# Input rows of the last 27 expert tiles turned by a DMA instead of TensorE and VectorE

## What is computed

```python
def _L1_ffn_ref(x, Wr, Wg, Wu, Wd):
    logits = jnp.einsum('bsd,de->bse', x, Wr)
    topk_w, topk_idx = jax.lax.top_k(jax.nn.softmax(logits, axis=-1), 2)
    ...
    gate = jax.nn.silu(jnp.einsum('th,ehi->tei', xf, Wg))
    hidden = gate * jnp.einsum('th,ehi->tei', xf, Wu)
    out = jnp.einsum('tei,eih,te->th', hidden, Wd, cw)
...
x = x + _L0_ffn_ref(_L0_cond_ref(x, ...), ...)
x = x + _L1_ffn_ref(_L1_cond_ref(x, ...), Wr, Wg, Wu, Wd)
```

## Time and profile before

| | |
|---|---|
| median of 3 runs | 653.41 us (652.63 to 1040.96) |
| the profiled execution | 653.3 us |
| its span in the trace | 651.6 us |
| TensorE's granted clock over the span | 0.971 of full speed |

### The profile page before, as it was taken

How to read it: one execution, slowest core, us unless ns; L and a number is a source line. 1 busy time by engine, 2 the same in 40 slices (tenths; PEclk the granted TensorE clock), 3 DMA queues, 4 the chain that set the end, 5 groups by cost and what they waited for, 6 DMA issues and landing times.

```text
span 651.6 us, 15669 instructions
## 1 busy us (share of the span) xinstructions
PE 599.1 (92%) x4478; PEld 412.9 (63%) x4482; DVE 505.2 (78%) x1336; ACT 438.3 (67%) x744; POOL 441.8 (68%) x596
## 2 busy tenths in 40 slices
PE   7989889998974488999999999999999999999995
PEld 2243336776752255777777777776777777777774
DVE  5579994888887888898988888888776666666653
ACT  3768997998945457788777878777665444455542
POOL 4115560287876996888877788878888676666544
PEclk8998999999996598999999999999999999999998
DMA  8622001346449147999999999977996666666662
GB/s 260 216 54 86 1 1 50 98 151 214 139 129 323 36 104 173 219 198 189 203 171 182 175 164 191 215 108 126 138 159 116 116 111 112 108 107 116 100 92 34
DMA packets 149378, 89.35 MB, mean 137 GB/s; under 512 B 106788, under 2 KB 142260, under 8 KB 149300
## 3 DMA queue, kind: packets, MB, share of 16 engines
q1 hardware_dynamic: 134596, 68.77, 47.2%
q0 software_dynamic: 14080, 19.54, 18.5%
q10 hardware_dynamic: 624, 0.03, 0.1%
HBM read 44.68 MB, written 18.40 MB: 97 GB/s over the span
## 4 chain that ended last, share of the span: by engine, by line
PE 60%; DVE 14%; POOL 7%; issue 6%; ACT 5%; DMA 4%; SPq 2%; POOLq 1%; DVEq 0%; ACTq 0%
PE ps L691 32%; PE ps L742 17%; POOL big L1675 3%; DMA small<-in_xT 2%; PE ps L670 2%; PE ps L547 2%; DVE small L1190 2%; DVE big L1545 2%; PE ps L542 1%; PE ps L565 1%; PE ps L637 1%; DMA small<-rows,small 1%; POOL big L1694 1%; DVE small L1258 1%; DMA big<-in_low 1%
## 5 line engine op out<-in xcount | busy, mean ns | idle before, releaser
L691 PE MATMUL ps<-big,small 128*128 x1608 | 251.7, 313 | 1.9 <-ACT small L973 1.3
L691 PEld LDWEIGHTS ps<-big,small 128*128 128x128 f16 x1608 | 156.9, 98 | 80.4 <-issue 4.0
L1726 POOL DMA_INDIRECT out<-small x67 | 107.4, 1603 | 74.8 <-DVE small L1512 70.9
L742 PE MATMUL ps<-big,small 128*128 x1105 | 131.3, 273 | 0.1
L742 PEld LDWEIGHTS ps<-big,small 128*128 128x128 f16 x1105 | 105.3, 98 | 11.5 <-issue 0.3
L979 ACT ACTIVATE small<-small 128x704 f16<-128x704 f32 x67 | 52.6, 785 | 77.0 <-DVE small L1487 76.4
L1503 DVE SCALAR_TENSOR_TENSOR small<-small 128x64 f16<-128x64 f32 (+1 forms) x134 | 72.6, 583 | 20.5 <-ACT small L983 20.5
L1694 POOL DMA_INDIRECT small<-rows,small x67 | 76.4, 1140 | 11.0 <-issue 10.8
L1487 DVE SCALAR_TENSOR_TENSOR small<-ps,small 128x704 f32<-128x704 f32 x67 | 63.5, 947 | 24.1 <-PE ps L691 21.7
L983 ACT ACTIVATE small<-small 128x704 f16<-128x704 f32 x67 | 59.1, 882 | 28.1 <-DVE small L1497 28.1
L1702 POOL TENSOR_SCALAR small<-small 128x1 f32<-128x1 f32 x67 | 69.6, 1038 | 0.0
(11 more groups left out here) (261 smaller groups left out, 1056.7 us busy)
## 6 DMA issues: line engine op xcount, KB each, us to landing
big<-in_Wg SPq DMA_DIRECT2D x8, 704.0 KB, 5.0
big<-in_Wu SPq DMA_DIRECT2D x8, 704.0 KB, 8.8
big<-in_Wd SPq DMA_DIRECT2D x8, 640.0 KB, 5.1
rows<-small SPq DMA_DIRECT2D x8, 518.0 KB, 5.0
big<-in_xT SPq DMA_DIRECT2D x8, 512.0 KB, 7.4
small<-in_xT SPq DMA_DIRECT2D x16, 256.0 KB, 4.4
out<-big SPq DMA_DIRECT2D x16, 256.0 KB, 3.9
small<-rows,small POOLq DMA_INDIRECT x67, 3.1
```

The source lines that it names most:

```text
L691: m = e.matmul(ps[:, 2 * j + h, 0:352], xsT_(t)[:, 2 * xp + k, :], bigh[:, bass.ds(o + (4 * j + 2 * wp + k) * I + 352 * h, 352)], start=(n ...
L742: m = e.matmul(ps[:, 7, 0:H], hTE_(t)[:, hc_, :], bigh[:, bass.ds(o + 8 * I + (6 * wp + c) * H, H)], start=(n == 0), stop=(n == len(terms) ...
L1726: e.indirect_dma_start(out=out[:, :], out_offset=bass.IndirectOffsetOnAxis(ap=IT[:, t:t + 1], axis=0), in_=yw_(t), in_offset=None, compute ...
```

## The change

From tile 45 on (`XD`) the input block is no longer turned by TensorE. A new function on SP, `turn_x(t)`, issues a DMA that turns the 128 x 512 block `xh` straight into `xsT`, four squares of 128 x 128. It waits for both halves of the block and for the up product of the tile three before, whose buffer it takes over. In the loop it stands two tiles ahead and before the turn of the hidden block. `turn_rows` and `evac_rows` stop after tile 44. There are three buffers of turned rows instead of two, and the third lies where the zero rows `padT` lay. Whoever waited for the turned rows, or for TensorE's having read `xh`, waits from tile 45 on for the DMA's semaphore (`xd0` to `xd2`). Two alignments move later buffers by one word.

```diff
+XD = 45
...
-        xsT = [carve(small, a, [4, P], F16) for _ in range(2)]
+        a[0] += -a[0] % 8
+        xsT = [carve(small, a, [4, P], F16) for _ in range(2)] + [carve(small, [pad_at], [4, P], F16)]
...
+        def rows_turned(t):
+            return ("xsT", t + 1) if t < XD else (f"xd{t % 3}", 16 * ((t - XD) // 3 + 1))
+
+        def rows_read(t):
+            return ("xp", t + 1) if t < XD else rows_turned(t)
...
+            def turn_x(t):
+                w.wait_ge("xhi", t + 1)
+                w.wait_ge("xlo", t + 1)
+                w.wait_ge("up", t - 2)
+                e.dma_start_transpose(out=xsT_(t), in_=xh_(t).rearrange("p a n -> p (a n)")).then_inc(S[f"xd{t % 3}"], 16)
...
+                if XD <= t + 2 < TILES:
+                    turn_x(t + 2)
                 if 0 <= t - 1 < TILES - BY_PE:
                     turn_hid(t - 1)
...
-                w.wait_ge("xsT", t + 1)
+                w.wait_ge(*rows_turned(t))
                 w.wait_ge(("sg", "hid")[j], t)
...
-                if 0 < t < TILES - 1:
+                if 0 < t < XD - 1:
                     turn_rows(t + 1)
...
-                w.wait_ge("xp", t - 1)
+                if t >= 2:
+                    w.wait_ge(*rows_read(t - 2))
...
             def evac_rows(t):
                 w.wait_ge("xp", t + 1)
-                w.wait_ge("up", t - 1)
+                w.wait_ge("up", t - 2)
+                if t >= SOLO:
+                    w.wait_ge("pad", PADS)
...
-                if t + 1 < TILES:
+                if t + 1 < XD:
                     evac_rows(t + 1)
```

More of the change, by code:

```diff
@@ L105, in build_program @@
         WrS = carve(small, a, [2, E])
+        a[0] += -a[0] % 8
+        pad_at = a[0]
         padT = carve(small, a, [PAY])
@@ L221, in build_program @@
         xhe = [carve(big, eb, [2, H], F16) for _ in range(2)]
-        xsTe = [carve(big, eb, [4, P], F16) for _ in range(2)]
+        xsTe = [carve(big, eb, [4, P], F16) for _ in range(3)]
         hide = [carve(big, eb, [I]) for _ in range(2)]
@@ L249, in build_program @@
                  "pm perm first tb slotF offI turnI oneof U hsc lo xlo xsT hid hsc2 hlo2 yw wc w "
-                 "pq lh hot slots ix it st0 st1 st2 st3 add0 add1 xk0 xk1 xst0 xst1 xst2 par0 par1 par2 hT0 hT1 hT2 xs0 xs1 xs2 xs3 xs4 "
+                 "pq lh hot slots ix it st0 st1 st2 st3 xd0 xd1 xd2 add0 add1 xk0 xk1 xst0 xst1 xst2 par0 par1 par2 hT0 hT1 hT2 xs0 xs1 xs2 xs3 xs4 "
                  "tgh tgl gvs gvv hl0 hl1 hl2 hl3").split()
@@ L706, in turn_gated_lo @@
                 w.wait_ge("pos", NB)
-                w.wait_ge("xsT", TILES)
+                w.wait_ge("xsT", XD)
                 w.wait_ge("gvs", 2 * late)
```

## The result

The changed kernel takes 647.7 us (median of 4 runs, 646.54 to 647.99) against 653.34 us for the kernel before. The medians differ by 5.6 us (0.9%). The ratio, which leaves out one slow run of the kernel before (1040.96 us), is 0.9903, with a 95% interval of 0.9881 to 0.9924: a gain of 0.8 to 1.2%, or 5.0 to 7.8 us. The forecast was 647.5. The profiled execution took 646.54 us, with a span of 644.9.

The account below looks back on a forecast made before the run. TensorE alone was taken to set the pace from 478.6 to 631.6 us. Span 651.6 - 5.9 = 645.7 us; plus 1.7 for execution over span, 647.4, and 0.1 to the median, 647.5 us; range 645 to 652.5.

Parts of the forecast that it names:

- The main step: Four turning products leave TensorE's path in each of 27 rounds, 0.22 us a round: 5.9 us less.
- The upper reading of 0.39 us a round: Time from the four products' first start to last end, taken as all saved: 27 x 0.39 = 10.5 us, upper end.
- VectorE's copy: VectorE loses 27 copies of 417 ns, 11.3 us of its time; nothing waits for it, so counted as nothing.
- The other edits: Loosened copy wait, third buffer, buffers moved by a word: zero, between -0.5 and +0.5 us.
- The new turn: Input block's DMA turn on SP's queue: lands in 1.9 to 3.6 us with 8.1 us available, so hidden.
- The hidden block's turn: Turn behind the new one on SP: lands in about 3.6 to 4.5 us, wanted 8.5 us after it goes out.
- The transfer: DMA engines' time for the input's 4 squares, by proportion from 1.87 us for 11: 0.68 us a round.
- The first rival: Turns of SP's queue don't overlap; the second begins when the first has landed: 9.2 us more, 662.5 us; chance 0.08.
- The second: Rival: busier DMA engines make TensorE wait now and then, 4.3 us over 147 us, so 651.7 us; chance 0.12.
- The third: Rival: the 0.22 us stays because TensorE's sequencer or another engine is just behind: 653.3 us; chance 0.04.
- The figure of 1309 ns a square: Rule against the change: 15 squares by DMA would take 19.6 us in each round, 376 us more.

Follow-up runs that it names:

- the kept products: Changed kernel, but TensorE also does four unread turning products of the identity matrix per round from tile 45 on: 653.73 us against 654.33 for the kernel before.
- the repeats: The changed kernel measured again unaltered, against the kernel before: 648.14 us against 653.82, ratio 0.9911, and in another set 646.9 us, ratio 0.991.
- the layout alone: Changed kernel with `XD = 72`, no tile turned by DMA; buffers, moved addresses and loosened waits stay: 653.88 us against 653.82 for the kernel before.
- forced: Changed kernel, but on SP each turn waits until the turn before it has landed: 690.48 us against 654.33 for the kernel before, ratio 1.0542.
- the kernel from 8: Changed kernel with `XD = 8`, all tiles from 8 on turned by DMA: 646.48 us, ratio 0.9904 to the kernel before.
- three extra turns: Changed kernel with three more unread turns of each input block, two of 4 squares and one of 2: 698.42 us against 653.34 for the kernel before.

## Why the prediction was right

The main step, 27 times 0.22 us on TensorE's path, is shown by the kept products: putting them back brings the time back to that of before. The upper reading of 0.39 us a round did not come; a round lost 0.22, the distance between starts, and not the 0.39 from the first start of the four products to their last end.

The count was slightly off. Rounds 44 and 45 together did not get shorter (in the repeats 44 gained 0.11 us and 45 lost 0.10). In 45 TensorE waits for the SiLU, as the timeline of the changed kernel shows:

```profile
482.47 1.58 ACT L977 ACTIVATE big<-small 128x1536 f16<-128x1536 f32 x1 [1.32 <-DVE small L1395]
...
484.08 1.82 DVE L1406 SCALAR_TENSOR_TENSOR big<-small,big 128x1536 f16<-128x1536 f32 x1 [0.48 <-ACT big L977]
...
486.38 0.88 ACT L1002 ACTIVATE small<-small 128x704 f16<-128x704 f32 x1 [1.26 <-DVE small L1519]
...
487.17 0.83 ACT L992 ACTIVATE small<-ps,small 128x704 f32<-128x704 f32 x1
...
488.24 1.96 PE L709 MATMUL ps<-big,small 128*128 x12 [0.49 <-ACT small L992]
```

The last piece of weights is converted there, on ScalarE (L977) and then VectorE (L1406). The hidden block's scale waits behind that, then its high half (L1002), then the SiLU. In the kernel before the turning products filled most of that wait. TensorE did save its 0.22 us in each of the two rounds, and gave it back here: its next 24 products, with the wait among them, take 4.40 us (485.80 to 490.20), and in the kernel before 3.85. So the path lost 25 x 0.22 = 5.5 us; I had read TensorE's busy time of that stretch and not what would be late next in its first two rounds. Medians differ by 5.6, 5.7 and 6.4 us in three measurements. That the forecast of 647.5 came within 0.2 us of the median is luck: the count was 0.4 us too high, and the same kernel took 648.1 and 646.9 in the other two.

VectorE's copy cost nothing, as said: the kernel that keeps it is as fast. The other edits cost nothing that shows, as said: the layout alone has a ratio of 1.0013 (0.9994 to 1.0033).

The new turn: the landing was expected between 1.9 and 3.6 us and is 3.3 in the median, 5.5 at most; the slowest is beyond what was expected, but inside the 8.1 us allowed. The hidden block's turn landed after 3.7 us in the median and 5.8 at most (the repeat, 478 to 626 us), where 3.6 to 4.5 were expected and some 8 allowed. SP's issue is not in proportion to the size: 1.19 us for 4 squares, 1.39 for 11. The transfer was put too low: q1 took 33.1% of 80 us for 14.1 turns, and in the changed kernel 56.7% of 80 us for 14.7 rounds, which is 3.1 us a round in place of 1.9: 1.2 more for the input's turn, and not 0.68. A second turn of the same block, in the kernel that turns it twice, added 0.85 (72.4% of 80 us), so 1.2 is what the turn added here and not its price everywhere. Nothing hung on it; the share came out at 0.83 for the 0.81 forecast. The queue between 520 and 600 us, in the changed kernel and in the one that turns each input block twice:

```profile
q1 hardware_dynamic: 29583, 7.33, 56.7%
```

```profile
q1 hardware_dynamic: 36608, 9.03, 72.4%
```

The first rival did not occur. Its main price, 9.2 us over the kernel before, was far too low, since it took 2.4 us for an input turn that lands after 3.3: forced, the loop took 36 us more than before. The second, TensorE losing time as the DMA engines fill, is refuted well beyond what was asked: even at a share of 0.99 the rounds stayed at 5.44 us, but for one of 5.53. The third, something just behind TensorE, is false for 25 rounds and true for two taken together, and in the kernel from 8, which gained 2.8 us of the 8.1 counted, for a good part of the earlier ones. The figure of 1309 ns a square from the Trainium skill ("VectorE: DVE Perf Modes", section "The three transpose paths") does not add up by square here: 4 squares land in 3.3 us and 11 in about 3.6. (In the prediction's sum with it, 27 x 14 is 378, not 376; nothing rests on that.)

## What to carry to other kernels

Moving small work off the engine that sets the pace gains the distance that it put between two starts, and gains it only in the rounds where that engine ends last; look round by round for what comes next before counting a round. A transfer that takes longer than the work it replaces cost nothing here, because its result was wanted later than it landed at its slowest: compare the longest landing, not the median, with the slack, and issue it as soon as its data are there. Count the time that each issue occupies on the queue's engine as well as the transfer: with five issues a round SP paced this loop while the DMA share was 0.90.

## What the runs showed of the hardware

A DMA share of 0.99 did not slow the loop, and 0.90 went with the slowest loop of all: the share did not tell the limit, and the queue's issues did, at medians of 1.2 to 1.5 us a turn, nearly the same for 4 squares (1.19) as for 11 (1.39). Two turns of one queue overlapped; making each wait for the one before cost 42 us. And where TensorE often waited the granted clock fell: to 0.94 in the stretch with three extra turns (busy for 92.62 of 110 us), where it was 1.00 in the changed kernel. How much of the 7.36 us that explains was not separated.
